# The buffers of a two-sublayer kernel moved to multiples of 2048 bytes, and LN2's squares written to another buffer

## The reference

```python
mod = (silu(c) @ wmod).reshape(4, 6, 1, 512)           # six rows per sequence
sa, ca, ga, sb, cb, gb = mod                            # ga, gb: size at least 0.25
h = layernorm(x) * (1 + ca) + sa
# attention sublayer: a linear recurrence over time with 128 states
omega, zeta, F = softplus(h @ W_omega.T + b), sigmoid(h @ W_zeta.T + b), h @ W_B.T + b
xs = scan(step, omega, zeta, F)                         # step: a damped rotation plus F
x = x + ga * (xs @ C.T + h @ D_mat.T)
h = layernorm(x) * (1 + cb) + sb
# FFN sublayer: each token is mixed with the one before it
xr, xk = mu_r * h + (1 - mu_r) * h_prev, mu_k * h + (1 - mu_k) * h_prev
x = x + gb * sigmoid(xr @ W_r.T) * (relu(xk @ W_k.T) ** 2 @ W_v.T)
```

## Time and profile before

| | us |
|---|---|
| median of 3 runs | 976.72 (976.17 to 977.73) |
| profiled execution, its own time | 977.14 |
| its span, first to last instruction | 975.4 |
| TensorE busy | 935.9 (96%), 5012 matmuls |
| weight loads busy | 786.9 (81%) |
| VectorE busy | 820.9 (84%) |
| ScalarE busy | 691.5 (71%) |
| GpSimd busy | 93.5 (10%) |
| mean granted clock of TensorE | 0.981 |

### The profile page before, as it was taken

How to read it: one execution, slowest core, us unless ns; L and a number is a source line. 1 busy time by engine, 2 the same in 40 slices (tenths; PEclk the granted TensorE clock), 3 DMA queues, 4 the chain that set the end, 5 groups by cost and what they waited for, 6 DMA issues and landing times.

```text
span 975.4 us, 14746 instructions
## 1 busy us (share of the span) xinstructions
PE 935.9 (96%) x5012; PEld 786.9 (81%) x5012; DVE 820.9 (84%) x2280; ACT 691.5 (71%) x1354; POOL 93.5 (10%) x117
## 2 busy tenths in 40 slices
PE   9995979899999999999999999999999999998997
PEld 3574858788888888888888888888888888887886
DVE  4897779898989989898998979898997989697562
ACT  4979765768777686777868686877768677765451
POOL 0001010001100202010200101110110201000000
PEclk9997998999999999999999999999999999999999
DMA  9820311020211312021121312021131201111001
GB/s 327 280 56 23 109 34 53 12 98 23 87 55 44 99 44 70 18 87 44 57 85 44 98 32 77 23 87 45 44 98 44 98 6 39 44 44 44 23 22 44
DMA packets 35275, 64.78 MB, mean 66 GB/s; under 512 B 3704, under 2 KB 4344, under 8 KB 35200
## 3 DMA queue, kind: packets, MB, share of 16 engines
q1 hardware_dynamic: 35200, 63.84, 19.8%
HBM read 47.02 MB, written 16.81 MB: 65 GB/s over the span
## 4 chain that ended last, share of the span: by engine, by line
PE 83%; DVE 8%; ACT 6%; issue 1%; DMA 1%; DVEq 0%; SPq 0%; ACTq 0%
PE ps_kr L328 32%; PE ps_cd L328 20%; PE ps_tv L328 18%; PE ps_pt L328 7%; PE ps_tv L369 3%; PE ps_pt L336 3%; ACT mix_full L734 1%; DMA stage_out<-in_wd 1%; DVE mix_full L985 1%; PE ps_cd L376 1%; DVE tmp L1206 1%; ACT x_in L600 1%; DVE state L1210 1%; PE ps_tv L389 0%; DVE tmp L1130 0%
## 5 line engine op out<-in xcount | busy, mean ns | idle before, releaser
L985 DVE SCALAR_TENSOR_TENSOR mix_full<-ps_tv,cur_m,mix_full 128x256 f32<-128x256 f32 x256 | 119.1, 479 | 37.7 <-ACT mix_full L734 37.6
L756 ACT ACTIVATE kk<-ps_kr 128x512 f32<-128x512 f32 x64 | 38.1, 599 | 123.4 <-PE ps_kr L328 123.1
L734 ACT ACTIVATE mix_full<-ps_tv,cur_m 128x255 f32<-128x255 f32 x256 | 120.0, 573 | 1.8 <-PE ps_tv L369 1.8
L1484 POOL TENSOR_SCALAR var<-sq 128x2 f32<-128x2 f32 (+1 forms) x34 | 37.1, 1091 | 642.5 <-ACT square_out L582 642.5
L328 PE MATMUL ps_kr<-mix_k_hi,wk_hi 128*128 128x256 f32 x512 | 80.9, 281 | 8.2 <-issue 8.2
L328 PEld LDWEIGHTS ps_kr<-mix_k_hi,wk_hi 128*128 128x128 f32 x512 | 71.2, 191 | 11.2 <-issue 8.8
L328 PE MATMUL ps_kr<-mix_k_hi,wk_lo 128*128 128x256 f32 x512 | 80.1, 279 | 0.0
L328 PE MATMUL ps_kr<-mix_k_lo,wk_hi 128*128 128x256 f32 x512 | 80.0, 279 | 0.0
L328 PE MATMUL ps_kr<-wr_hi,mix_r_hi 128*128 128x512 f32 x256 | 71.5, 402 | 5.5 <-ACT kk L756 5.5
L328 PE MATMUL ps_tv<-wv_hi,kk_hi 128*128 128x512 f32 x256 | 72.8, 408 | 0.8 <-issue 0.8
L328 PE MATMUL ps_kr<-wr_hi,mix_r_lo 128*128 128x512 f32 x256 | 69.9, 395 | 0.0
(11 more groups left out here) (213 smaller groups left out, 2239.6 us busy)
## 6 DMA issues: line engine op xcount, KB each, us to landing
x<-in_x SPq DMA_DIRECT2D x32, 512.0 KB, 3.7
out<-x SPq DMA_DIRECT2D x32, 512.0 KB, 2.8
x_in<-in_x SPq DMA_DIRECT2D x15, 1024.0 KB, 5.1
x<-in_wmod SPq DMA_DIRECT2D x3, 1024.0 KB, 7.6
mix_full<-in_wmod SPq DMA_DIRECT2D x2, 1024.0 KB, 9.1
x_in<-in_x SPq DMA_DIRECT2D x2, 512.0 KB, 5.7
stage_out<-in_wd SPq DMA_DIRECT2D x1, 1024.0 KB, 10.0
stage_mix<-in_wmod SPq DMA_DIRECT2D x1, 1024.0 KB, 10.5
```

The lines of the kernel that those rows point to most:

```text
L734: mm = act.activation(mix[n][:, k, 1:UNIT], ps_tv[:, j, c * UNIT:(c + 1) * UNIT - 1], ACT.Identity, bias=cur_m[:, SHIFT + k:SHIFT + k + 1] ...
L756: act.activation(kk[:, i, :], ps_kr[:, i, :], ACT.Relu).then_inc(s_relu, 1)
L985: dve.scalar_tensor_tensor(mix[n][:, k, :], ps_tv[:, j, c * UNIT:(c + 1) * UNIT], cur_m[:, alpha + k:alpha + k + 1], mix[n][:, k, :], ALU. ...
L1484: pool.tensor_scalar(var[:, :], sq[:, :], 1.0 / D, EPS, ALU.mult, ALU.add).then_inc(s_var, 1)
```

## The change

All tensors of 2048 bytes or more are declared first, behind a filler of 896 bytes (224 fp32 numbers), so that each starts on a multiple of 2048 bytes: first the operands of TensorE, then the buffers of the other engines, then the small tensors. What lies over a staging area before does so after. The scratch `square_out2` (bf16) is gone; `statistics2` gives `squares` the buffer xn2 instead (rt for unit 1), which is fp32, and `squares` waits for an earlier square only where the scratch is square_out1.

```diff
+        sb("to_2048", [P, 224])
         proj = [sb(f"proj_{n}", [P, KC, 256], F32R) for n in ("hi", "lo")]
...
         wv = [sb(f"wv_{n}", [P, KC, D], F32R) for n in ("hi", "lo")]
+        h = [[sb(f"h_{n}{i}", [P, KC, CHUNK], F32R) for n in ("hi", "lo")] for i in range(2)]
+        xss = [sb(f"xs_{m}", [P, CHUNK], F32R) for m in ("hi", "lo")]
+
+        with nc.sbuf_tensor("stage_mix", [P, 2, KC, D], F32) as stage_mix:
+            pass
+        mixs = [[sb(f"mix_{n}_{w}", [P, KC, UNIT], F32R) for w in ("hi", "lo")] for n in "kr"]
+        with nc.sbuf_tensor("stage_kk", [P, KC, D], F32) as stage_kk:
+            pass
+        kks = [sb(f"kk_{m}", [P, KC, UNIT], F32R) for m in ("hi", "lo")]
+        with nc.sbuf_tensor("stage_out", [P, KC, D], F32) as stage_out:
+            pass
+        xn2 = sb("xn2", [P, TPU, D])
+        rt = sb("rt", [P, TPU, D])
+        kk = sb("kk", [P, 2, 2 * UNIT])
+        x_in = sb("x_in", [P, TPC, D])
+        h_full = sb("h_full", [P, KC, CHUNK])
+        x2 = sb("x2", [P, 4, TPU, D])
+        mix_full = sb("mix_full", [P, 2, KC, UNIT])
+        mix = [mix_full[:, n] for n in range(2)]
+        xs = sb("xs", [P, CHUNK])
+        gate_a = sb("gate_a", [P, D])
+        gate_b = sb("gate_b", [P, D])
+        square_out1 = sb("square_out1", [P, 2, D], mybir.dt.bfloat16)
+
         ident = sb("ident", [P, P])
...
-        square_out1 = sb("square_out1", [P, 2, D], mybir.dt.bfloat16)
-        square_out2 = sb("square_out2", [P, 2, D], mybir.dt.bfloat16)
...
             def squares(x, neg_mean, scratch, out, count, s_sq):
                 for i in range(out.shape[1]):
-                    if count + i >= 2:
+                    if scratch is square_out1 and count + i >= 2:
                         act.wait_ge(s_sq, count + i - 1)
                     act.activation(scratch[:, i % 2, :], x[:, i, :], ACT.Square, bias=neg_mean[:, i:i + 1],
                                    accum_out=out[:, i:i + 1]).then_inc(s_sq, 1)
...
-                squares(x2[:, u % 4], neg_mean2[:, u % 2], square_out2, sq2[:, u % 2], u * TPU, s_sq2)
+                squares(x2[:, u % 4], neg_mean2[:, u % 2], rt if u == 1 else xn2, sq2[:, u % 2], u * TPU, s_sq2)
```

More of the change, by code:

```diff
@@ L67, in build @@
         cur_m = sb("cur_m", [P, NTAB])
-        gate_a = sb("gate_a", [P, D])
-        gate_b = sb("gate_b", [P, D])
         minus_half = sb("minus_half", [P, TPC])
-        x_in = sb("x_in", [P, TPC, D])
         gate_cols = sb("gate_cols", [P, 3, 2, B * D // P])
@@ L80, in build @@
         bn = sb("bn", [P, TPC, 2])
-        square_out1 = sb("square_out1", [P, 2, D], mybir.dt.bfloat16)
-        square_out2 = sb("square_out2", [P, 2, D], mybir.dt.bfloat16)
         rstd1 = sb("rstd1", [P, TPC])
-        h_full = sb("h_full", [P, KC, CHUNK])
-        h = [[sb(f"h_{n}{i}", [P, KC, CHUNK], F32R) for n in ("hi", "lo")] for i in range(2)]
-        x2 = sb("x2", [P, 4, TPU, D])
         sum2 = sb("sum2", [P, 2, TPU])
@@ L93, in build @@
         last_n = sb("last_n", [P, KC])
[L94 to L108, removed]
         om_pos = sb("om_pos", [P, HALF])
@@ L120, in build @@
         state = sb("state", [P, 3, HALF + 1])
-        xs = sb("xs", [P, CHUNK])
-        xss = [sb(f"xs_{m}", [P, CHUNK], F32R) for m in ("hi", "lo")]
         x2_a, x2_b = (x2[:, i:i + 2].rearrange("p a t n -> p (a t) n") for i in (0, 2))
```

## The result

The change made the kernel slower. Fifteen runs of each: before 977.22 us median (976.17 to 978.03), after 980.23 us (978.70 to 981.38), a ratio of 1.0032 with the interval 1.0024 to 1.0039: 3.0 us lost where 4.7 were forecast as gained.

The account below looks back on a forecast made before the run. The prediction took TensorE's matmul spacings as the bound for some 700 of 975 us. Its terms gave 5.2 us, less 0.5 for the ends: 4.7 off 977.14 is 972.4, or 972.0 for the median; range 966 to 981.

Parts of the forecast that it names:

- The stationary operand's start modulo 128 sorts them; the moving operand does not: TensorE's matmul spacings: stationary operand at 0 gives 226.7 ns per 512 columns, at 64 229.2, at 96 233.3.
- (a): r and v products, 64 in 32 units: each goes from 5.50 to 5.44 us, 3.8 us gained.
- (b): States part, six matmuls: 1.40 to 1.36 us, 0.04 in each of 31 units, 1.2 us gained.
- (c): k products: 30 of 32 at the floor of 5.47 us, two late ones at 5.66; 0.2 us gained.
- Rival 3: TensorE's products slower because stationary and moving operand start at the same place: 999 us; chance 0.15, in full or half.
- Rival 1: No change: the 2.5 ns of r and v has another source and stays; 976.7 +-1 us, chance 0.14.
- rival 2: All TensorE products also regain the lost sixteenth, blamed on starts at 64 or 128 modulo 256: 926 us, chance 0.06.
- (d): TensorE's transposes, 0.87 us for 8, paced by the weight load: at most 4 ns each either way, taken as 0.
- squares: 64 LN2 Squares on ScalarE, now writing fp32 to xn2: 715 ns each, change taken as 0, bounds 6 us either way.
- start and end: Landings and ScalarE's passes at both ends: +-1 us, taken as 0; a half-clock stretch more or less: +-3.4 us.

Follow-up runs that it names:

- e3: Changed kernel, but mix_k and wk both start at 64 bytes, mix_r and wc at 32; single execution 986.32 us, kernel before 977.63.
- e4: Changed kernel, but mix_k starts at 1024 bytes, mix_r at 128, xs at 32; single execution 984.00 us, kernel before 977.63.
- e2: Changed kernel, but mix_k starts at 128 bytes, wr at 64, xs and wc both at 96; single execution 984.16 us, kernel before 977.63.
- e1: Changed kernel, but mix_k starts at 64 bytes, mix_r and wr both at 64, xs at 96; single execution 978.09 us, kernel before 977.63.
- h1: Changed kernel, but wk starts at 64 bytes, kk_hi/kk_lo at 192, xs_hi/xs_lo at 96; seven executions 974.38 us, kernel before 977.42, ratio 0.9971.
- f4: Changed kernel, but mix_k starts at 32 bytes; single execution 975.88 us (before 976.90), in eleven 977.04 against 977.40, ratio 0.9996.
- f1: Changed kernel, but wk starts at 64 bytes, mix_r at 256; single execution 977.12 us, kernel before 976.90.
- f3: Changed kernel, but wk starts at 576 bytes, mix_r at 512; single execution 976.33 us, kernel before 976.90.
- g1: Changed kernel, but wk starts at 64 bytes, kk_hi/kk_lo at 192; single execution 976.25 us, kernel before 977.03.

## Why the prediction was wrong

**What bounds the kernel: right.** TensorE's spacings set the time between 200 and 890 us before and after; all of the loss is a change of spacing.

**"The stationary operand's start modulo 128 sorts them; the moving operand does not": wrong, and the root of the miss.** For matmuls of 512 columns the distance between the two operands modulo 256 sorts the steady spacings: 0, 256, 512 give 226.7 ns; 64 and -64 give 229; -32 and 128 give 233.3 and 232.7 (r in e3 and e4). For 32 and -96 there are only the states' six matmuls, 233 each on the mean, and e2 shows that so short a part costs 1.39 us at distance 0 too. The earlier trace rows fitted both readings, because all weights start at one place, 1152. The one product that didn't fit the distance was k, at -64 and on the floor; that should have kept it open, but the prediction used it to rule the distance out ("the moving operand does not sort them: k's moving one is at 64 and pays nothing").

**(a) r and v, 3.8 us, and (b) states, 1.2 us: right in sign, by luck of the rule, and (a) too large.** The alignment also brought every distance to 0; e1, e2 and e4 show for r that it is the distance that pays. r and v gave 2.8 us and not 3.8, because the 0.06 of the even units was taken for all 64 products: behind transposes v is slow for its first ten matmuls with aligned operands too, and gained 0.02. The states gave 1.1.

**(c) k, "at the floor", 0.2 us gained: the step that failed.** It lost 8.0 us (0.28 in each steady unit) where a gain of 0.2 was forecast: the term was taken from a "floor" that was none. Being at 0 modulo 128 was not why k was at 113.3. k, with 256 columns and a weight load for each, obeys another list: distance 0, 96, 128 or 1024: 120.0 ns; -32: 118.3; 32: 116.7; 64 or -64: 117.8 or 113.3, depending on what runs ahead. The kernel before had the good rhythm at k's distance of -64, behind a v at 64 and states at -96; h1 puts just these three back, with everything else aligned, and has it again. The 5.66 of the earlier trace rows, which the prediction called "a second way for the weight load and the matmul to mesh" and weighed at 0.2 us, was the sign in the rows that k's spacing wasn't a floor of its own but a state that a layout can lose.

**Rival 3 had the sign, and for k the condition.** "Stationary and moving operand at the same place" costs k 120.0 where it priced 118 (0.56 us per two units, priced 0.45). That the memory serves one of them first, its reason, no run shows, and 96 or 128 bytes apart cost k the same 120.0. It also held for k alone: for matmuls of 512 columns the same place is the best one, which is why its 999 did not come. Its bounds let the range hold the result; its chance of 0.15 was too small for a kernel of which 1536 of 5012 matmuls are k's. The "steps of 512 bytes make no difference now" held against it was true (all are multiples of 256) but no argument about 0 against 64.

**Rule.** The prediction weighed a rule by which all placements read alike and took the trace's side, rightly: with mix_k alone moved by 32 bytes k takes 116.7 ns for 120.0 (f4). The Trainium skill (SBUF — State Buffer, Who interferes with whom) says "PE and ACT never wait on anyone". That sentence is about contention between engines, which no run here tests; it doesn't speak of one engine's own two operands, and it gives no ground to expect that their places don't matter.

**Rival 1** was dead by (a) and (b); **rival 2** too: with all at 0 modulo 2048 a 512-column matmul still takes 226.7 ns.

**(d), squares, start and end: right.** Transposes stayed at 0.87 us for 8 (the piece at 526.84 in the chain of after), the squares at 716 ns, VectorE and ScalarE at their old sums. Both profiled executions have stretches at half clock of 6.8, 6.8, 10.2, 3.4 and 6.8 us at the same points of the program (and one in the last 5 us), and the mean granted clock is the same.

**Open.** What in the memory or the engine makes the distance count isn't shown; only distances and rhythms were varied. Why the product ahead selects between 113.3 and 117.8, why k's list of distances differs from the 512-column one, why a product needs up to ten matmuls to settle, and why k products of h1 at either end (at 186 and 931 us when timed) still took 5.66 was not settled. Whether accesses of the other engines have a part was not varied by itself.

## What to carry to other kernels

Where TensorE is never idle, compare the spacing of each kind of matmul, start to start, with the best one of its shape, and look at the distance between its stationary and moving operand modulo 256 rather than at the alignment of each. Before calling a spacing a floor, look for the same product at another spacing in the same trace: two rhythms mean that the good one can be lost. Don't multiply a gain read in one unit by all units before looking at each kind of unit: here v gained 0.06 us in even ones and 0.02 in odd ones. A layout is cheap to vary, so move one pair at a time: aligning everything lost 3.0 us, and with two deliberate offsets of 64 bytes the kernel took 4.8 less than before, at least 3.2 of them from the spacings.

## What the runs showed of the hardware

- A matmul of 512 fp32r columns at full clock takes 226.7, 229 or about 233 ns once its product has settled, by the distance of its operands' starts modulo 256 (r in after, e1 to e4, f1 to f3).
- Behind a product of another placement, or behind transposes, it takes up to some ten matmuls to settle: v with both operands at 0 took 5.44 us behind aligned states, 5.48 behind states at 96 (e2) and 5.49 behind transposes.
- A matmul of 256 such columns, with a weight load for each, takes 113.3, 116.7, 117.8, 118.3 or 120.0 ns; 120.0 comes at distance 0, where the 512-column one is fastest, and at 96 and 128.
- At 64 bytes' distance the same product with the same operands had two rhythms, 113.3 and 117.8 ns, each held to the end of the product once reached (g1). Which of them came changed with the placement of operands that only the products ahead of it use (kk, xs).
